# Rotary projection with components on partitions, and a four-head ring of q and k filled by transfers inside SBUF

## What is computed

```python
def _apply_rope(x, cos, sin):
    xr = x.reshape(x.shape[:-1] + (-1, 2))
    xe, xo = (xr[..., 0], xr[..., 1])
    c = cos[None, :, None, :]
    s = sin[None, :, None, :]
    return jnp.stack([xe * c - xo * s, xe * s + xo * c], axis=-1).reshape(x.shape)
c_q = _rmsnorm(x @ Wq_down, q_norm_w)                 # 48 latents
q = (c_q @ Wq_up).reshape(b, s, H, HD).transpose(0, 2, 1, 3)
q_rope = _apply_rope((x @ Wq_rope).reshape(b, s, H, RD), cos, sin)
c_kv = _rmsnorm(x @ Wkv_down, kv_norm_w)              # 64 latents
k = (c_kv @ Wk_up).reshape(b, s, H, HD).transpose(0, 2, 1, 3)
v = (c_kv @ Wv_up).reshape(b, s, H, HD).transpose(0, 2, 1, 3)
k_rope = _apply_rope((x @ Wk_rope).reshape(b, s, H, RD), cos, sin)
scores = (jnp.einsum('bhqd,bhkd->bhqk', q, k) + jnp.einsum('bhqd,bhkd->bhqk', q_rope, k_rope)) * scale
attn = jax.nn.softmax(scores, axis=-1)
out = jnp.einsum('bhqk,bhkd->bhqd', attn, v)
```

## Time and profile before

| | |
|---|---|
| median of 3 runs | 1313.69 us (1313.36 to 1316.0) |
| the profiled execution's own time | 1315.61 us |
| its span | 1313.1 us |
| PE busy | 1011.6 us (77%), 7949 instructions |
| DVE busy | 743.4 us (57%) |
| POOL busy | 668.8 us (51%) |
| ACT busy | 584.3 us (45%) |
| DMA, mean over the span | 69 GB/s |

### The profile page before, as it was taken

One profiled execution on the slowest core, in us unless ns is written; L12 is line 12 of the kernel. 1 busy time (PEld: TensorE's weight loads), 2 busy tenths in 40 slices (PEclk: granted clock), 3 DMA queues, 4 the chain that ended last, 5 costly groups with the idle time before them and its releaser, 6 DMA issues.

```text
span 1313.1 us, 25564 instructions
## 1 busy us (share of the span) xinstructions
PE 1011.6 (77%) x7949; PEld 841.8 (64%) x7950; DVE 743.4 (57%) x1730; ACT 584.3 (45%) x1099; POOL 668.8 (51%) x782
## 2 busy tenths in 40 slices
PE   4688888978978988988988978844311989999960
PEld 3566766766767767767767767643310879999950
DVE  5685554555645645645646646665400666666657
ACT  1224664655556656656656646601100433444420
POOL 4324665655646655656656656530575003555544
PEclk9688999999989999989989989955655899999985
DMA  5620201102002002002002002045232003333335
GB/s 183 227 80 4 84 2 52 36 2 86 1 2 86 1 2 86 1 2 86 1 2 86 2 19 69 1 181 152 77 117 94 0 19 106 116 117 117 115 117 229
DMA packets 42815, 90.76 MB, mean 69 GB/s; under 512 B 6063, under 2 KB 31030, under 8 KB 40206
## 3 DMA queue, kind: packets, MB, share of 16 engines
q1 hardware_dynamic: 35814, 71.56, 16.8%
q0 software_dynamic: 6912, 17.84, 3.8%
HBM read 51.36 MB, written 40.11 MB: 70 GB/s over the span
## 4 chain that ended last, share of the span: by engine, by line
PE 50%; DVE 17%; issue 13%; ACT 7%; another core or an unknown queue 5%; POOL 5%; DMA 1%; DVEq 0%; POOLq 0%; ACTq 0%; SPq 0%
PE bank L600 9%; PE bank L602 8%; PE bank L601 8%; PE bank L1005 5%; DVE nmax L1204 4%; POOL p_lo L1730 4%; ACT p_f L1542 3%; PE bank L715 3%; PE bank L775 3%; DVE qT L1180 3%; PE bank L750 3%; PE bank L721 3%; ACT qT L1524 2%; PE bank L911 2%
## 5 line engine op out<-in xcount | busy, mean ns | idle before, releaser
L1730 POOL TENSOR_TENSOR p_lo<-p_f,p_hi 128x512 f16<-128x512 f32 x259 | 301.4, 1164 | 252.0 <-ACT p_f L1542 252.0
L1537 ACT ACTIVATE p_hi<-bank,log_up 128x512 f16<-128x512 f32 x259 | 178.4, 689 | 160.6 <-PE bank L602 154.1
L1542 ACT ACTIVATE p_f<-bank,log_up 128x512 f32<-128x512 f32 x259 | 177.1, 684 | 0.0
L1204 DVE TENSOR_REDUCE nmax<-bank 128x1 f32<-128x512 f32 x264 | 169.3, 683 | 6.9 <-PE bank L750 6.2
L775 PE MATMUL bank<-vals,p_hi 128*128 x2048 | 141.7, 195 | 39.5 <-POOL p_lo L1730 20.8
L775 PEld LDWEIGHTS bank<-vals,p_hi 128*128 128x128 f16 x2048 | 112.1, 98 | 76.9 <-issue 70.6
L1180 DVE TENSOR_TENSOR qT<-bank,qT 128x512 fp32r<-128x512 f32 x66 | 45.6, 692 | 194.0 <-ACT qT L1524 193.9
L775 PE MATMUL bank<-vals,p_lo 128*128 x1024 | 123.3, 194 | 0.0
L600 PE MATMUL bank<-qT,kT 128*128 128x512 f32 x259 | 115.2, 445 | 0.0
L715 PE MATMUL bank<-ident,qk_tok 128*128 128x128 f32 x528 | 86.5, 289 | 30.8 <-DVE qT L1180 29.5
L750 PE MATMUL bank<-kT,qT 128*128 128x512 f32 x264 | 100.0, 449 | 9.6 <-DVE nmax L1204 7.2
(11 more groups left out here) (237 smaller groups left out, 2517.3 us busy)
## 6 DMA issues: line engine op xcount, KB each, us to landing
slots<-pad SPq DMA_DIRECT2D x8, 1440.0 KB, 10.7
h<-slots SPq DMA_DIRECT2D x80, 144.0 KB
h_st<-h_dram SPq DMA_DIRECT2D x8, 1024.0 KB, 5.9
w_hi<-parts SPq DMA_DIRECT2D x16, 512.0 KB, 7.6
w_raw<-in_w SPq DMA_DIRECT2D x4, 1408.0 KB, 10.2
h_dram<-h_hl SPq DMA_DIRECT2D x3, 1024.0 KB, 4.9
w_p<-in_w SPq DMA_DIRECT2D x1, 2816.0 KB
xa<-in_x SPq DMA_DIRECT2D x4, 512.0 KB, 7.1
```

The costliest lines, as they stand in the source:

```text
L1204: dve.tensor_reduce(nmax[:, k % MAXES:k % MAXES + 1], max_bank[q % 2][:], AX_X, ALU.max, negate=True)\
L1537: act.activation(p_hi[:, u % TB, :], score_bank[u % 2][:], ACT.Exp, bias=log_up[:, 0:1], scale=SCALE)
L1542: act.activation(p_f[:, u % 2, :], score_bank[u % 2][:], ACT.Exp, bias=log_up[:, 0:1], scale=SCALE)\
L1730: pool.tensor_tensor(p_lo[:, u % TB, :], p_f[:, u % 2, :], p_hi[:, u % TB, :], ALU.subtract).then_inc(s_pl, 1)
```

## The change

`qT` and `kT`, and the token-major buffer `qk_tok` before them, go. A ring `qk` of four heads holds q and k of a head as [component, high or low, token], a pair of heads in each half. Work is prepared for a pair of heads (8 units), two pairs ahead:

- `pr` is now two tasks for a pair (even, odd components): the weights are the stationary operand, 512 tokens the moving one, and the result is on partitions as 32 components x (q of head 0, q of head 1, k of head 0, k of head 1). Six matmuls of 512 columns each.
- DVE multiplies each by cosine and sine (`turn`, four operations of 128 x 512 for a pair), POOL subtracts and adds (`rotate`, two operations of 128 x 512), ACT and DVE make high and low parts into `eo_hl`.
- `kl` replaces `ab`: three matmuls of 512 columns give the key latents of both heads on partitions, split into `kl_hl`.
- SP copies them into the ring in 12 transfers for a pair (`fill`): 2 of the query latents (48 partitions), 2 of the key latents (48 partitions), 8 of the rotary parts (32 partitions), each row 4 KB. It first waits until the scores of the pair that used this half are done (`s_score`), and the first `score_max` of the new pair waits for all 12 (`filled`).
- `tq`, `tk` and their copies are gone. `score_max` runs once in every unit, 8 units ahead. The batch's latents are stored and loaded for 128 partitions (`lat_st`, two of them). ACT waits for the previous `fill` before it writes the staging buffers again (`staging_free`).
- The loop has 4 iterations of 64 units. The pads are written once in an iteration, twice as much each time. In the prologue `value_weights` comes ahead of the maxima, and the second half of the ring can be filled only after the `mout` matmuls (`m_mm`), since the weights for them lie in it.

The core of the diff:

```diff
-IT_HEADS = 2 * GH
-UNITS = IT_HEADS * TB
-ITERS = NB * H // IT_HEADS
+UNITS = H * TB
+PAIRS = H // 2
 AHEAD = 3
+MAX_AHEAD = 2 * TB
+RING = 4
+FILLS = 12
...
-    for s in range(IT_HEADS):
+    for s in range(H):
         at[TB * s].append(("sh", s + 1))
-        at[TB * s].append(("tq", s + 2))
-        at[TB * s + 1].append(("tk", s + 2))
...
+    for p in range(PAIRS):
+        at[8 * p].append(("pr", 0, p + 2))
+        at[8 * p + 1].append(("pr", 1, p + 2))
+        at[8 * p + 2].append(("kl", p + 2))
+        at[8 * p + 5].append(("ot", p - 1))
+    for g in range(PAIRS // 2):
         for n in range(2):
+            at[16 * g + 7 + n].append(("op", g - 1, n))
...
+        qk = sb2("qk", [P, RING, 2, 2, SEQ], F32R)
...
+            def fill(i, r):
+
+                done, base = filled[r % 2], 2 * (r % 2)
+                par = 0 if i is None else prep_batch(i, r) % 2
+                if i is None:
+                    sp.wait_ge(*((m_mm, 4) if r else (wr_l, 1)))
+                else:
+                    sp.wait_ge(s_score, UNITS * i + 8 * (r - 1))
+                latents = lat_st[KL:LATENTS].bitcast(F32).rearrange("p z a t -> p z (a t)")[:, bass.ds(par, 1), :]
+                qk_f, eo_f, kl_f = qk[:].bitcast(F32), eo_hl[:].bitcast(F32), kl_hl[:].bitcast(F32)
+                for h in range(2):
+                    sp.dma_start(qk_f[SPARE:RD, base + h, 0].rearrange("p a t -> p (a t)").unsqueeze(1), latents).then_inc(done, 16)
+                sp.wait_ge(s_kll, pair_count(i, r) + 1)
+                for h in range(2):
+                    sp.dma_start(qk_f[SPARE:RD, base + h, 1], kl_f[h * KL:h * KL + QL]).then_inc(done, 16)
+                for w in range(2):
+                    sp.wait_ge(s_eol, 2 * pair_count(i, r) + w + 1)
+                    for x in range(2):
+                        for h in range(2):
+                            rows = slice(RD + 32 * w, RD + 32 * (w + 1))
+                            of = slice(32 * (2 * x + h), 32 * (2 * x + h + 1))
+                            sp.dma_start(qk_f[rows, base + h, x], eo_f[of, w]).then_inc(done, 16)
...
                     for c in range(KD):
+                        mm = mm3(dst[:], wr_hi[:, c, g, of], wr_lo[:, c, g, of],
+                                 h_st[:, 0, c, :], h_st[:, 1, c, :], c == 0, c == KD - 1)
...
+                    mm = mm3(dst[:], ab_hi[:, g * P:(g + 1) * P], ab_lo[:, g * P:(g + 1) * P],
...
+            def score_max(i, k):
+
+                s, q = k // TB, k % TB
+                if q == 0 and s % 2 == 0:
+                    pe.wait_ge(filled[(s // 2) % 2], fills(i, s // 2))
...
+            with pe.Fori(0, NB) as i:
                 for u in range(UNITS):
                     weigh_values(i, u)
-                    for s, q in maxes_at(u):
-                        score_max(i, s, q)
+                    score_max(i, u + MAX_AHEAD)
+                    for t in AUX_AT[u]:
+                        if t[0] == "sh":
+                            aux(i, AUX_K[t], t)
                     score(i, u + AHEAD)
+                    for t in AUX_AT[u]:
+                        if t[0] != "sh":
+                            aux(i, AUX_K[t], t)
...
+                dve.tensor_tensor(turns[:, w, w], src[:], trig_s[:, 0], ALU.mult)
+                dve.tensor_tensor(turns[:, w, 1 - w], src[:], trig_s[:, 1], ALU.mult).then_inc(s_turn, 1)
...
+                dve.tensor_tensor(eo_hl[:, w, 1, :], turns[:, 0, w], eo_hl[:, w, 0, :].bitcast(F32), ALU.subtract)\
...
+                dve.tensor_tensor(kl_hl[:, 1, :], aux_home(i, k)[:], kl_hl[:, 0, :].bitcast(F32), ALU.subtract).then_inc(s_kll, 1)
...
+                    if u % 8 == 3:
+                        low_rotary(i, r, 0)
+                    if u % 8 == 4:
+                        low_rotary(i, r, 1)
+                        low_latents(i, AUX_K[("kl", r)], r)
...
+                    if u % 8 == 2:
+                        staging_free(i, r)
+                        high_rotary(i, r, 0)
+                    if u % 8 == 3:
+                        high_rotary(i, r, 1)
+                        high_latents(i, AUX_K[("kl", r)], r)
...
+                pool.wait_ge(s_turn, 2 * pair_count(i, r) + 2)
+                pool.tensor_tensor(turns[:, 0, 0], turns[:, 0, 0], turns[:, 1, 0], ALU.subtract).then_inc(s_eo, 1)
+                pool.tensor_tensor(turns[:, 0, 1], turns[:, 0, 1], turns[:, 1, 1], ALU.add).then_inc(s_eo, 1)
```

More of the change, by code:

```diff
@@ L399, in aux_tasks, with prep_batch, out_slot @@
                     k += 1
[L401 to L418, removed]
-        def out_slot(i, par):
-            return (i + 1) // 2 if par else i // 2 + 1
+        AUX_K = {t: k for u, k, t in aux_tasks()}
+        def prep_batch(i, r):
+            return i if r < PAIRS else (i + 1) % NB
+        def out_slot(i, g):
+            return i if g < 0 else i + 1
         Z_LOOP = range(2, NT - 4)
@@ L533, in _ @@
                 sp.wait_ge(q, 32)
-            last = max(k for u, k, t in aux_tasks() if t[0] in ("pr", "ab") and t[1] == 1)
             sp.wait_ge(pad_set, 3)
-            with sp.Fori(0, ITERS) as i:
-                sp.wait_ge(aux_done, aux_count(i, last))
-                stage(((i + 1) // 2) % NB)
+            with sp.Fori(0, NB) as i:
+                sp.wait_ge(filled[0], fills(i, 0))
+                sp.wait_ge(filled[1], fills(i, 1))
+                sp.wait_ge(aux_done, aux_count(i, 0))
+                stage_latents((i + 1) % NB, (i + 1) % 2)
+                for r in range(2, PAIRS - 1):
+                    fill(i, r)
+                sp.wait_ge(aux_done, aux_count(i, AUX_K[("pr", 1, PAIRS - 1)]))
+                stage_inputs((i + 1) % NB)
+                for r in range(PAIRS - 1, PAIRS + 2):
+                    fill(i, r)
                 sp.dma_start(slots[bass.ds(i * (PADS * P), PADS * P)].rearrange("(s p) n -> p s n", p=P),
                              pad[:].unsqueeze(1).to_broadcast([P, PADS, XW])).then_inc(padded, 16)
-            sp.wait_ge(staged, 32 * ITERS)
-            sp.wait_ge(s_x, 4 * ITERS + 4)
+            sp.wait_ge(staged_h, 16 * NB)
+            sp.wait_ge(staged_l, 16 * NB)
+            for z in range(2):
+                sp.wait_ge(filled[z], 16 * FILLS * (NB * PAIRS // 2 + 1))
+            sp.wait_ge(s_x, PAIRS * NB + 4)
             for b in range(NB):
@@ L1254, in second_statistics @@
                 ins.then_inc(f_stat, 1)
[L1257 removed]
+            dve.wait_ge(s_x, PAIRS * NB + 2)
             second_statistics(0, NB - 1)
[L1259 to L1264 removed]
+            low_outputs(NB, 0, -1)
+            gated(NB, 1, LAST[1])
+            gated(NB, 2, LAST[2])
+            dve.wait_ge(s_x, PAIRS * NB + 4)
+            dve.wait_ge(s_norm, H * NB + 2)
             second_statistics(NB - 1, NB)
+            for z in range(2):
+                dve.wait_ge(filled[z], 16 * FILLS * (NB * PAIRS // 2 + 1))
             for b in range(NB):
@@ L1545, in _ @@
             act.wait_ge(p_cst, 16 * (NB - 1))
-            for k, t in enumerate(AUX_FIRST):
-                aux(None, k, t)
-            act.wait_ge(log_set, 1)
-            for u in range(AHEAD):
-                exponentials(None, u)
+            high_latents(None, 2, 0)
+            for w in range(2):
+                high_rotary(None, 0, w)
+            staging_free(None, 1)
+            high_latents(None, 5, 1)
+            for w in range(2):
+                high_rotary(None, 1, w)
             for q in mb_st:
@@ new lines, in add_rows, with spare_rows @@
+            def add_rows(i, t):
+                _, g, n = t
+                c = op_count(i, g, n)
+                pool.wait_ge(s_yg, c + 1)
+                pool.wait_ge(s_x, c + 2)
+                pool.tensor_tensor(idle[:, 1:2], mhalf[:, 0:1], mhalf[:, 0:1], ALU.add)
+                rows = xa[:, bass.ds(out_slot(i, g) * TB + 2 * n, 2), :]
+                pool.tensor_tensor(rows, rows, y_gate[:, n], ALU.add).then_inc(s_x, 1)
+            def spare_rows(z):
+                of = qk[:, 2 * z:2 * z + 2].bitcast(F32)
+                pool.memset(of[0:SPARE], 0.0).then_inc(spare_c, 1)
+                pool.wait_ge(spare_c, z + 1)
+                pool.memset(of[0:1, :, 1, 0, :], 1.0).then_inc(spared, 1)
```

499 lines of the change are left out of this document (223 added, 276 removed).

## The result

The changed kernel takes 1399.19 us in the median of its runs (1397.39 to 1400.4) against 1313.53 us (1310.12 to 1316.0) for the kernel before in the same series: a ratio of 1.0653 with a 95% interval of 1.0626 to 1.068. It is slower by 86 us, where 46 were forecast. The profiled execution has a span of 1398.0 us at a mean granted clock of 0.851.

The account below looks back on a forecast made before the run. Bound: a chain of PE work 11.3, transfer 11.1 and clock loss 2.2, 24.6 us a pair against 23.2. Loop 783.4 us, 40 more; with 6 for the prologue, 1361.6 profiled, so 1360 us median; range 1285 to 1415.

Parts of the forecast that it names:

- the cycle: Loop, from one fill's landing to the next: PE work plus transfer, 22.4 us at full clock, 24.6 with slow clock.
- Transfer part: From the end of the pair's last score to PE's restart after the fill lands: 11.1 us, of which 8.9 data.
- Issues: Twelve transfer starts on SP per fill: 0.47 us each, 5.6 us in all, hidden under the data.
- The chain of low parts: Work making high and low parts before the key latents' transfers: hidden, no cost; 1 us later would add 1 us a pair.
- PE part: PE's work from a fill's landing to the end of the last score that frees the ring half: 11.3 us.
- The clock: PE work after each stall runs at the lower clock level: 2.2 us lost a pair.
- PE's stall: PE idle before the first `score_max` of each pair, waiting for the fill: 5.5 us a pair.
- Borders and prologue: Iteration borders add about 1 us in all; the loop starts about 6 us later, between 0 and 12.
- the clock staying up: Rival: the loop's stall is there but the clock does not drop; 22.4 us a pair, 1290 us; chance 0.17.
- Full-width rates: Rival: ring transfers run as fast as full-width ones; 19.1 us a pair, about 1195 us; chance 0.07.
- The slower transfers: Rival: transfers inside SBUF need 12 us of data (153 GB/s); 27.7 us a pair, 1456 us; chance 0.14.
- a PE-bound loop: If PE stayed the bound: 16.9 us of PE work a pair, the loop about 5 us a pair shorter.

Follow-up runs that it names:

- rows32: Changed kernel with the four 48-partition latent transfers of a fill made as six of 32 partitions, same bytes: 1385.36 us.
- early_kl: Changed kernel with the key latents' transfers reading query latents, without waiting for the key latents' low part: 1398.64 us.
- fewer: Changed kernel with the eight rotary transfers of a fill made as five, same bytes, nine issues instead of twelve: 1394.58 us.
- half: Changed kernel with the same twelve transfers carrying only high parts in the loop, 2 KB rows instead of 4 KB: 1338.11 us.
- warm: Changed kernel with 18 unread 512-column matmuls on PE ahead of each wait for the fill: 1352.33 us, ratio 1.0292 to the kernel before.
- mid: Changed kernel with the first maximum of each head one unit later (units 1, 2, 2 and 3): 1238.68 us, ratio 0.941 to the kernel before.

## Why the prediction was right, and where its sizes were off

The direction, the place and the form were right: 31 waits of `score_max` in every eighth unit, ended by a DMA, clock dips in every pair (0.90 over the loop, forecast 0.85 to 0.93), about 210 GB/s at the end of fills (forecast 200 to 220), no idle time of its own at the borders. 1360 was forecast and 1399 measured, within the range of 1285 to 1415. That range is wide: the loss itself, 86 us, is nearly twice the 46 forecast. The error is one of sizes, in the cycle: 25.97 us for 24.6, and 31 x 1.37 = 42 us is all of it (39). By its terms, for the cycle from 215.32 back to the score before it and on to the next:

- *Transfer part*, forecast 11.1: measured 12.0, from the end of the last score (203.29, its last matmul at 203.06 and the 0.23 us that one takes) to 215.32. This is the term that was sized too small. Its data part took 9.7 us (from about 204.6 to 214.3 by its 1-us stretches, which hold 1.87 MB in all, 192 GB/s), not 8.9. I had rested it on the 215 GB/s of 64-partition stores, scaled to all engines busy, and kept the mean with their gaps, 175 GB/s, for the upper end; the truth lies between. By the stretches about half of the excess is in the first 393 KB, the query latents up to 207, at 164 GB/s with the gap; the rest moves at 202. The 0.8 us a pair, 25 us in all, are most of what was missing. What they are made of is shown in part only: 32 partitions for 48 gave back 0.38 us (`rows32`), closing the gap alone nothing (`early_kl`). The Trainium skill, SBUF — State Buffer, section "Door 1: The DMA port swizzle", has a partition table by which the prediction worked out an estimated 9.7 us; it quoted that and did not sum by it, having no row for it. The trace agrees in size, though the 9.7 us that it shows hold the gap as well. Fixed parts were 2.1 us (203.49 to 204.6, 214.3 to 215.32) for 1.7 and 0.1.
- *Issues*, forecast 0.47 us each and hidden. They take 0.59 in the median, twelve of them with the gap 9.6 us in the cycle shown (203.49 to 213.06). Hidden still (`fewer`: 4.6 us in all), but with less to spare than thought; `half` shows that they take over as soon as the bytes shrink.
- *The chain of low parts*, costed at nothing with the warning that 1 us later would cost 1 us a pair. It was later: SyncE waits 1.2 us for the key latents. The reason is in one group of the page:

```profile
L1185 DVE TENSOR_TENSOR eo_hl<-turns,eo_hl 128x512 fp32r<-128x512 f32 x68 | 88.4, 1302 | 0.0
```

  VectorE's subtraction takes 1.30 us, not the 0.7 that I took from a product that reads PSUM; it reads two tiles in SBUF while GpSimd works there too. The same instruction in the prologue, with GpSimd idle, and in the loop (start, us; two in the first row):

```profile
79.09 1.28 DVE L1185 TENSOR_TENSOR eo_hl<-turns,eo_hl 128x512 fp32r<-128x512 f32 x2
203.70 1.63 DVE L1185 TENSOR_TENSOR eo_hl<-turns,eo_hl 128x512 fp32r<-128x512 f32 x1
```

  The four of the prologue take 0.68 us each, the 64 of the loop 1.05 to 1.64. The rotary low parts stand ahead of the key latents' on VectorE (201.58 and 203.70 for 205.25). The zero came out right all the same, and the warning of 1 us a pair wrong: `early_kl` takes the wait away and gains nothing. Why is open. In the changed kernel the queue does move less at 206, 127 GB/s against 180 in `early_kl`; but there the transfers behind lost that again (176 and 160 GB/s at 207 and 208 against 209 and 188), and they all read the same partitions.
- *PE part*, forecast 11.3 + 2.2 for the clock, of which 0.71 is a mean share of `op`: 12.8 for this cycle, which has none. Measured 13.1 (215.32 to 228.42). A lone `score_max` takes 0.32 (201.85 to 202.16 is 0.31), not half of a pair; five of them make 0.25 of the 0.3 that are over.
- *The clock*, forecast 2.2 a pair: the matmuls between 215.32 and 220.1 run at the lower level, about half of 4.8 us lost. `warm` gives at least 1.5 and `mid` about 2.1. Right.
- *PE's stall*, forecast 5.5, measured 4.8 on average: PE's work under the transfer, with its own short waits, was longer than 5.6 (6.5 in the cycle shown, 203.29 to 209.8).
- *Borders and prologue.* Cycles that hold a border take 27.2 to 27.8 us, 1 to 2 more than their neighbours, three times, where 1 us in all was forecast: some 4 us. The loop starts at 113.35, 6.5 us later than the earlier trace rows, forecast 6.

The rivals: the clock staying up is refuted twice, by the rows and by `warm`, which with the clock up is still slower than before; its 22.4 us a pair were too few, for the transfer's sake. Full-width rates did not occur in the fill shown (225 GB/s at most in a stretch of 1 us). The slower transfers (12 us of data) came closest to what happened, at a quarter of their excess.

What the prediction did not ask is how small the remedy is. It wrote that the wait stands in unit 8(r-1) and the last score in unit 8(r-1)-4, and worked out a PE-bound loop some 5 us a pair shorter; it took the wait's place as given. Each unit by which the first maximum is put off takes its work out of the chain: 5.27 us a pair for the first unit, and 1.28 for the second, where the chain (20.7 less 2.5, the unit's score, `pr` and `weigh_values`) falls below PE's own 19.4 and stops mattering.

## What to carry to other kernels

Where a buffer is released by one instruction and asked for by another that stands a few units behind it in the same engine's order, the transfer between them is not hidden by a busy engine: add up landing, release, fill, landing as a chain, and compare it with the engine's own work per round. If it is longer, first look at whether the asking instruction can stand later; here moving the maxima by two units turned a loss of 6.5% into a gain of 8.9%, with no byte less transferred. A stall that recurs and lowers TensorE's clock each time costs more than itself, here a third to a half as much again (1.5 to 2.2 us beside 4.8). Most of that went as the stall shrank in `mid`, so here the first microseconds taken off it were worth the most.

## What the runs showed of the hardware that I had not expected

- An issue on SyncE of a transfer within SBUF takes 0.59 us whether it carries 64 or 128 KB (`half`, changed kernel), and 1.1 us for the third and fourth of four transfers of 192 KB issued without a pause (`early_kl`: 2.18 us for two).
- Four transfers of 48 partitions back to back, all from the same ones, move at 160 to 180 GB/s (`early_kl`). The eight of 32 partitions move at 193 to 213 in the full stretches of a fill of `rows32`.
- How much of the lost clock came back with the first unit: 31 waits of 4.8 us at a granted clock of 0.90, 17 waits of up to 3.0 us at 0.97 (`mid`).
- Two SBUF operands on VectorE beside GpSimd: 1.05 to 1.64 us for 128 x 512 in the loop, against 0.68 for the same instruction with GpSimd idle and 0.69 with one operand in PSUM. The Trainium skill, SBUF — State Buffer, section "Who interferes with whom", has this rule: a VectorE instruction with two SBUF inputs contends with a GpSimd instruction that reads SBUF. The trace agrees: two SBUF operands alone cost nothing more, and with GpSimd at work all 64 are slower.
